# Queries, keys and values from three single-pass products of upper and lower parts instead of one full-precision product

## The reference

```
t = t + sliding_window_attention(_ln_t(t), Wq, Wk, Wv, Wo)   # 8 heads of 16, window 64
t = t + ternary_feed_forward(_ln_t(t), weight, bias)         # weight to its sign, output quantized
t = t + causal_attention(_ln_t(t), W_Q, W_K, W_V, W_O)       # 8 heads of 16
t = t + mixture_of_experts(_ln_t(t), ...)                    # 8 experts, 2 chosen for each token
```

## Time and profile before

| | |
|---|---|
| median of 3 runs | 248.85 us (248.84 to 248.93) |
| profiled execution | 249.03 us, of which the span is 247.2 us |
| TensorE busy (PE) | 230.5 us, 93% |
| VectorE busy (DVE) | 200.3 us, 81% |
| ScalarE busy (ACT) | 172.7 us, 70% |
| GpSimd busy (POOL) | 88.0 us, 36% |
| granted TensorE clock | full (2.4 GHz) throughout |

### The profile page before, as it was taken

One profiled execution on the slowest core, in us unless ns is written; L12 is line 12 of the kernel. 1 busy time (PEld: TensorE's weight loads), 2 busy tenths in 40 slices (PEclk: granted clock), 3 DMA queues, 4 the chain that ended last, 5 costly groups with the idle time before them and its releaser, 6 DMA issues.

```text
span 247.2 us, 4532 instructions
## 1 busy us (share of the span) xinstructions
PE 230.5 (93%) x1491; PEld 172.9 (70%) x1493; DVE 200.3 (81%) x524; ACT 172.7 (70%) x500; POOL 88.0 (36%) x155
## 2 busy tenths in 40 slices
PE   7999998899988989799897998999999999999993
PEld 2698666467765758466575666788888888888882
DVE  3677899966596897968799674889999996699885
ACT  2386455799698967998679976965855666666550
POOL 5200225988898556286288450002300000000000
PEclk9999999999999999999999999999999999999999
DMA  6910000004430300002000000510220002612001
GB/s 182 359 30 4 0 1 0 0 10 133 117 85 5 85 3 0 0 3 86 3 0 1 3 0 7 170 42 0 55 77 0 3 0 55 202 42 76 12 1 42
DMA packets 9318, 11.71 MB, mean 47 GB/s; under 512 B 704, under 2 KB 5952, under 8 KB 9168
## 3 DMA queue, kind: packets, MB, share of 16 engines
q1 hardware_dynamic: 8864, 11.09, 14.7%
q10 hardware_dynamic: 432, 0.33, 0.4%
HBM read 10.87 MB, written 0.56 MB: 46 GB/s over the span
## 4 chain that ended last, share of the span: by engine, by line
PE 62%; DVE 24%; ACT 8%; issue 2%; DMA 1%; POOL 1%; DVEq 0%; SPq 0%
PE bank L1006 6%; PE bank L1018 6%; PE bank L1007 6%; PE bank L1008 6%; PE bank L1019 6%; PE bank L1021 6%; DVE negmax L1146 5%; ACT early_prob L525 5%; PE bank L770 4%; PE bank L746 3%; PE bank L786 3%; DVE kM L1132 2%; DVE k_parts L1116 2%; DVE q_lo L1122 2%; PE bank L832 2%
## 5 line engine op out<-in xcount | busy, mean ns | idle before, releaser
L656 ACT ACTIVATE hb<-bank,pk 128x512 f32<-128x512 f32 x64 | 42.9, 706 | 20.6 <-PE bank L1008 20.6
L1401 DVE TENSOR_TENSOR hlo<-hb,hhi 128x512 fp32r<-128x512 f32 x64 | 43.1, 696 | 8.1 <-ACT hhi L659 7.0
L1146 DVE TENSOR_REDUCE negmax<-bank 128x2 f32<-128x384 f32 (+2 forms) x48 | 30.4, 641 | 13.0 <-PE bank L752 12.9
L525 ACT ACTIVATE prob<-bank,negmax 128x192 f32<-128x192 f32 (+1 forms) x64 | 28.2, 454 | 3.9 <-DVE negmax L1146 3.5
L486 ACT ACTIVATE probT<-bank 128x512 f32<-128x512 f32 x38 | 22.7, 610 | 4.3 <-PE bank L770 2.9
L1006 PE MATMUL bank<-xhi,w_hi 128*128 128x512 f32 x64 | 25.3, 396 | 0.0
L375 POOL TENSOR_TENSOR rstd<-ve,neghalf 128x2 f32<-128x2 f32 x16 | 11.4, 724 | 38.7 <-DVE ve L1103 38.7
L1018 PE MATMUL bank<-hhi,w_hi 128*128 128x512 f32 x64 | 25.1, 392 | 0.0
L1008 PE MATMUL bank<-xhi,w_lo 128*128 128x512 f32 x64 | 25.0, 390 | 0.0
L1007 PE MATMUL bank<-xlo,w_hi 128*128 128x512 f32 x64 | 25.0, 390 | 0.0
L1019 PE MATMUL bank<-hhi,w_lo 128*128 128x512 f32 x64 | 24.9, 389 | 0.0
(11 more groups left out here) (154 smaller groups left out, 516.8 us busy)
## 6 DMA issues: line engine op xcount, KB each, us to landing
w_raw<-w SPq DMA_DIRECT2D x16, 256.0 KB, 3.1
comb_b<-routes SPq DMA_DIRECT2D x16, 256.0 KB, 3.4
pk<-packed SPq DMA_DIRECT2D x1, 1280.0 KB, 8.4
pk<-packed SPq DMA_DIRECT2D x1, 560.0 KB, 5.7
xs<-x SPq DMA_DIRECT2D x3, 128.0 KB, 2.7
out<-acc SPq DMA_DIRECT2D x3, 128.0 KB, 1.7
xs<-x ACTq DMA_DIRECT2D x1, 128.0 KB, 2.9
out<-acc ACTq DMA_DIRECT2D x1, 128.0 KB, 1.8
```

The source lines that it names most:

```text
L525: last = nc.scalar.activation(prob_of(n, u)[:, of], lane[n][u % 2][:, of], ACT.Exp, bias=negmax[n][:, unit_query(u), h:h + 1], accum_out=s ...
L656: nc.scalar.activation(hb[blk % 2][:, j, :], h_bank[j][:, :], ACT.Relu, bias=bias).then_inc(h_ready, 1)
L1146: V.tensor_reduce(negmax[n][:, unit_query(u), heads[0]:heads[-1] + 1], lane[n][u % 2][:, :].rearrange("q (h k) -> q h k", h=len(heads))[:, ...
L1401: V.tensor_tensor(hlo[blk % 2][:, j, :], hb[blk % 2][:, j, :], hhi[blk % 2][:, j, :].bitcast(F32), ALU.subtract).then_inc(hlo_ready, 1)
```

## The change

1. The six projection weights leave `pk` and get a transfer of their own into a tile `projections` (128 x 2 x 640, 655 KB), on the SyncE queue behind the constants and ahead of the experts' weights.
2. GpSimd splits them into `p_hi` and `p_lo` in eight instructions of 128x320 between the group-norm powers of the first and of the second stage, waiting for the new transfer.
3. ScalarE's `turned` writes, for j = 0 and 2, the rounded tile `h_hi` in place of hT.
4. VectorE gets `lower_normed(a, n)`: bank minus h_hi, written to `h_lo`, 128x256, eight times. In phase 0 two stand around the copying of tokens 2 and 3, and two behind the first `largest` of both inputs (for inputs 2 and 3); in phases 2 and 3 two stand behind the last norm and ahead of `inverse_sums`.
5. TensorE's `project` does three F32R products for each full-precision one, 24 instead of 16 instructions for a pair, the third of each waiting for `h_lo`; the very first also waits for the split weights. `values` does three in place of one.
6. hT becomes two buffers instead of four; the first turn of probabilities in phase 0 waits for `h_low_ready` where it waited for `lnT_ready`.

```diff
@@ memory and loading
+        projections = sb("projections", [128, 2, QKV], scope=first_memory)
+        h_hi = each("h_hi", [128, T], F32R, n=2, scope=attention_memory)
+        h_lo = each("h_lo", [128, T], F32R, n=2, scope=attention_memory)
+        p_hi = each("p_hi", [128, QKV], F32R, n=2, scope=attention_memory)
+        p_lo = each("p_lo", [128, QKV], F32R, n=2, scope=attention_memory)
+            sp.dma_start(projections[:, :, :], packed[:, PACKED:].rearrange("p (a w) -> p a w", a=2)).then_inc(projections_in, 16)
@@ GpSimd
+            def split_projections(a):
+                for i in range(2):
+                    of = slice(i * QKV // 2, (i + 1) * QKV // 2)
+                    G.tensor_copy(p_hi[a][:, of], projections[:, a, of]).then_inc(p_upper, 1)
+                    pool.wait_ge(p_upper, 2 * a + i + 1)
+                    G.tensor_tensor(p_lo[a][:, of], projections[:, a, of], p_hi[a][:, of].bitcast(F32),
+                                    ALU.subtract).then_inc(p_ready, 1)
             for j in range(2):
+                if j == 1:
+                    pool.wait_ge(projections_in, 16)
+                    for a in range(2):
+                        split_projections(a)
                 for p, ns in enumerate(PAIRS):
@@ ScalarE, turned
-                copy(hT[n][:, :], norm_bank(j, n)[:, 0:T]).then_inc(lnT_ready, 1)
+                copy((h_hi[n % 2] if j in (0, 2) else hT[n % 2])[:, :], norm_bank(j, n)[:, 0:T]).then_inc(lnT_ready, 1)
@@ TensorE
             def project(a, n):
                 pe.wait_ge(lnT_ready, normed(2 * a, n))
-                for dst, w in ((lane[n][1], A_WK[a]), (lane[n][0], A_WQ[a])):
-                    for g in range(2):
-                        last = mm(dst[:, g * T:(g + 1) * T], w[:, g * 128:(g + 1) * 128], hT[n][:, :],
-                                  start=True, stop=True)
-                    last.then_inc(aqk_full, 1)
+                if a == 0 and n == 0:
+                    pe.wait_ge(p_ready, 4)
+                for bank_at, at in ((lane[n][1], WK_AT), (lane[n][0], WQ_AT)):
+                    projected(bank_at, a, n, at).then_inc(aqk_full, 1)
+            def projected(bank_at, a, n, at):
+                for g in range(2):
+                    upper, lower = parts_of(a, at + g * 128, at + (g + 1) * 128)
+                    sums = bank_at[:, g * T:(g + 1) * T]
+                    mm(sums, upper, h_hi[n % 2][:, :], start=True, stop=False)
+                    mm(sums, lower, h_hi[n % 2][:, :], start=False, stop=False)
+                    pe.wait_ge(h_low_ready[n], a + 1)
+                    last = mm(sums, upper, h_lo[n % 2][:, :], start=False, stop=True)
+                return last
             def values(a, n):
                 pe.wait_ge(k_parts_ready, a * B + n + 1)
+                upper, lower = parts_of(a, WV_AT, WV_AT + 128)
                 for i in range(TT):
-                    last = mm(lane[n][1][:, i * 128:(i + 1) * 128], hT[n][:, i * 128:(i + 1) * 128], A_WV[a],
-                              start=True, stop=True)
+                    of = slice(i * 128, (i + 1) * 128)
+                    mm(lane[n][1][:, of], h_hi[n % 2][:, of], upper, start=True, stop=False)
+                    mm(lane[n][1][:, of], h_hi[n % 2][:, of], lower, start=False, stop=False)
+                    last = mm(lane[n][1][:, of], h_lo[n % 2][:, of], upper, start=False, stop=True)
@@ turn_probs
-                    pe.wait_ge(lnT_ready, normed(0, other(n)))
+                    pe.wait_ge(h_low_ready[other(n)], 1)
@@ VectorE
+            def lower_normed(a, n):
+                dve.wait_ge(lnT_ready, normed(2 * a, n))
+                V.tensor_tensor(h_lo[n % 2][:, :], norm_bank(2 * a, n)[:, 0:T], h_hi[n % 2][:, :].bitcast(F32),
+                                ALU.subtract).then_inc(h_low_ready[n], 1)
             norm(0, 1)
+            lower_normed(0, 0)
             tokens(PAIRS[1])
+            lower_normed(0, 1)
             norm_variance(PAIRS[1])
             for p, (a, ns) in enumerate(PHASES):
                 if p >= 2:
                     norm(2, ns[1])
+                    for n in ns:
+                        lower_normed(1, n)
                 if p:
                     for n in ns:
                         inverse_sums(PHASES[p - 1][0], other(n))
...
                 for n in ns:
                     copy_values(a, n)
                     largest(a, n, 0)
+                if p == 0:
+                    for n in PAIRS[1]:
+                        lower_normed(0, n)
```

More of the change, by code:

```diff
@@ L29 @@
 BLOCKS = 2 * E
+QKV = 640
 RING = 4
@@ L37 @@
     group=128, vecs=8, wq=128, wk=128, wv=128, ident=128, wp=128, squeeze=96, conv=3 * 128,
-    aq=256, ak=256, av=128, ao=128, ident_bf=64, band0=64, band1=128, fw=128, fb=256, mean=128,
-    cq=256, ck=256, cv=128, co=128, causal0=64, causal1=128, headmask=8, router=8,
-    iota=8, b1=E * HC, b2=E,
+    ao=128, ident_bf=64, band0=64, band1=128, fw=128, fb=256, mean=128,
+    co=128, causal0=64, causal1=128, headmask=8, router=8,
+    iota=8, b1=E * HC, b2=E, aq=256, ak=256, av=128, cq=256, ck=256, cv=128,
 )
@@ L46 @@
     _at += _width
-PACKED = _at
+PACKED = AT["aq"]
 FIRST = AT["wq"]
-EARLY = AT["aq"]
+EARLY = AT["ao"]
 GAMMA, BETA, BQ, BK, BV, BP, BSQ, BCONV = range(8)
@@ L123, in build @@
         ht = each("ht", [128, TT, 128])
-        hT = each("hT", [128, T])
+        hT = each("hT", [128, T], n=2)
         fy = each("fy", [128, TT, 128], n=2)
@@ L216, in build @@
             sem(n) for n in ("av_full", "rb_ready", "rT_full", "rT_ready", "attn_ready", "wo_full", "t_ready"))
+        h_low_ready, p_upper, p_ready, projections_in = sems("h_low_ready"), sem("p_upper"), sem("p_ready"), sem("projections_in")
         unseen_zeroed = sems("unseen_zeroed")
@@ L235, in build, with parts_of @@
         y_full, yc_ready, acc_ready = sem("y_full"), sem("yc_ready"), sem("acc_ready")
-        A_WQ, A_WK, A_WV, A_WO = ([const(f"{layer}{n}") for layer in "ac"] for n in "qkvo")
+        A_WO = [const(f"{layer}o") for layer in "ac"]
+        def parts_of(a, lo, hi):
+            return p_hi[a][:, lo:hi], p_lo[a][:, lo:hi]
+        WQ_AT, WK_AT, WV_AT = 0, 256, 512
         A_MASK = [[const(f"{kind}{i}").bitcast(BF16) for i in range(TT)] for kind in ("band", "causal")]
@@ L390, in lower_tokens @@
                 pool.wait_ge(lnT_ready, normed(3, n))
-                G.tensor_tensor(xlo[:, cols], hT[n][:, :], xhi[:, cols].bitcast(F32), ALU.subtract
+                G.tensor_tensor(xlo[:, cols], hT[n % 2][:, :], xhi[:, cols].bitcast(F32), ALU.subtract
                                 ).then_inc(xlo_ready, 1)
@@ L702, in product @@
                     if j == 1:
-                        last = mm(lane[n][2][:, T + i * 128:T + (i + 1) * 128], hT[n][:, i * 128:(i + 1) * 128],
+                        last = mm(lane[n][2][:, T + i * 128:T + (i + 1) * 128], hT[n % 2][:, i * 128:(i + 1) * 128],
                                   w_eff[:, :], start=True, stop=True)
                     else:
-                        last = mm(logits_at(n)[:, i * E:(i + 1) * E], hT[n][:, i * 128:(i + 1) * 128],
+                        last = mm(logits_at(n)[:, i * E:(i + 1) * E], hT[n % 2][:, i * 128:(i + 1) * 128],
                                   const("router"), start=True, stop=True)
@@ L1506 @@
         mean=np.full((128, 128), 1.0 / C / C, f32),
-        cq=twice(a["L3_attn_W_Q"].reshape(128, 128).T), ck=twice(a["L3_attn_W_K"].reshape(128, 128).T),
-        cv=a["L3_attn_W_V"].reshape(128, 128).T, co=paired_rows(a["L3_attn_W_O"].T),
+        co=paired_rows(a["L3_attn_W_O"].T),
         causal0=mask(causal[0][:, 0:128]), causal1=mask(causal[1]),
@@ L1512 @@
         b1=a["L3_ffn_b1"].reshape(E * HC, 128).T, b2=a["L3_ffn_b2"].T,
+        aq=twice(a["L2_attn_Wq"].T), ak=twice(a["L2_attn_Wk"].T), av=a["L2_attn_Wv"].T,
+        cq=twice(a["L3_attn_W_Q"].reshape(128, 128).T), ck=twice(a["L3_attn_W_K"].reshape(128, 128).T),
+        cv=a["L3_attn_W_V"].reshape(128, 128).T,
     )
```

1 line of the change is left out of this document (removed).

## The result

The changed kernel takes 251.68 us (median of 4 runs, 251.60 to 251.72), the kernel before 248.84 (4 runs, 248.80 to 248.93): a ratio of 1.011 [1.0095, 1.0125], 2.84 us slower. The prediction was 251.1, range 249.2 to 253.8, slower with a chance of 0.80. The profiled execution took 251.68 us and has a span of 249.9 (247.2 before), so the two traces differ by 2.7.

What follows compares the result with a forecast made beforehand. VectorE's full stretches at attention phase boundaries were taken as the bound. Terms 0.4 + 0.85 + 0.6 + 0.6 - 0.2 gave +2.25 us, so 251.1 us was predicted, range 249.2 to 253.8.

Steps and rivals of the forecast that it cites:

- The bound: Attention phase boundaries: VectorE's full stretches set the end, so work put there counts and TensorE savings inside do not.
- The rival that TensorE bounds: Whole kernel: cheaper key and query products count and VectorE's work is hidden, -1.1, 247.8 us; chance 0.08.
- the rival of slack: VectorE's insertions: absorbed by later idle time, with phase 1's saving paying for the rest, 249.0 us; chance 0.12.
- The cost of a single-pass product: TensorE keys, queries and values: 0.11 us per instruction, so a key bank takes 0.18 less.
- The rival of values at four passes: TensorE values: six instructions of 0.22 us per input, +2.3 on top of the sum, 253.4 us; chance 0.20.
- Phase 0, start (+0.85): VectorE before phase 0's first lower_keys: two subtractions of 0.42 us for inputs 0 and 1 delay it by 0.85.
- Phase 0, after the first maximum (+0.6): VectorE between unit 0's and unit 1's maxima: two more subtractions, 0.84 less 0.24, delay it by 0.6 us.
- the same 0.24: Phase 0: gap between VectorE's maxima merge ending at 48.53 and ScalarE's unit-1 early_prob at 48.77, subtracted from 0.84.
- Phases 2 and 3 (+0.33, +0.3): VectorE before lower_keys: subtractions wait for ScalarE's copies with inverse_sums behind, +0.33 and +0.3, together +0.6 us.
- Phase 1 (-0.2): Phase 1 start, where VectorE idled for k_parts: the shorter first key bank counts in full, -0.2 us.
- The first part (+0.4): First 25 us: GpSimd's weight split meets VectorE's first_probs on SBUF, +0.4 us, bounds 0 and 1.2.

Runs made afterwards that it cites:

- no_lower_inputs: The changed kernel without VectorE's eight lower-part subtractions of the inputs and the product that reads them: 248.81 us, ratio 0.9985 to the kernel before.
- one_product: The changed kernel with all subtractions but only one of three products for keys and queries: 251.87 us, ratio 1.0124 to the kernel before.
- load_only: The kernel before with the six projection weights moved to a tile and transfer of their own, nothing split: 249.04 us, ratio 1.0004.
- split_only: The kernel before with the separate weight transfer and GpSimd's eight splitting instructions, whose results nothing reads: 249.12 us, ratio 1.0007.
- changed_again: The changed kernel run once more with no edit: 251.28 us, ratio 1.0095 to the kernel before.
- maxima_first: The changed kernel with phase 0's subtractions for inputs 2 and 3 each moved behind its lane's unit-1 maximum: 254.85 us, ratio 1.0227 to the kernel before.
- inverse_between: The changed kernel with the two inverse_sums of phases 2 and 3 put between the two subtractions: 250.87 us, ratio 1.0074 to the kernel before.
- clock_kept: The changed kernel with seven bf16 products of zeroes in TensorE's two gaps of phase 0: 251.73 us, ratio 1.0117 to the kernel before.
- between_kept: The changed kernel with seven zero products in phase 0's TensorE gaps and inverse_sums between the subtractions in phases 2 and 3: 250.68 us, ratio 1.0063.
- split_late: The changed kernel with GpSimd waiting for first_probs of inputs 0 and 1 before it splits the weights: 251.51 us, ratio 1.0095 to the kernel before.
- the second set: Four variants, the unedited changed kernel (251.28 us) among them, run on one chip with the kernel before at 248.97 us (11 runs).

## Why the prediction was right

**The bound.** Right. Taking VectorE's subtractions away, with the product that reads them, returned all of the loss (no_lower_inputs); taking away two of the three products for keys and queries and leaving the subtractions returned none (one_product), though there two falls of the clock hid 0.36 us of gain. The rival that TensorE bounds, 247.8 us, is dead by both, in spite of 93% busy. So is the rival of slack, 249.0: the subtractions stand on the chain.

**The cost of a single-pass product.** Right within a tenth: 0.12 us at 256 columns (0.11 taken, so a bank is 0.13 shorter by these distances and not 0.18) and 0.11 at 128. The rival of values at four passes, 253.4, falls by the three rows at 42.76 to 42.98. The loads last 0.19 and are 0.11 apart, so length was the wrong thing to price by and distance the right one, as the prediction read from the earlier trace rows. The rule of the Trainium skill that it weighed (TensorE: Matmul & The Clock Gate, section LDWEIGHTS: 107 ns for 128 columns) is the one that held as a pace: 0.11 and 0.12 us were measured.

**Phase 0, start (+0.85).** Measured +0.83, and 0.84 taken back by no_lower_inputs.

**Phase 0, after the first maximum (+0.6).** +0.46. Two subtractions in a row take 0.66 on the chain, not 0.84: the second starts 0.33 behind the first, before the first has ended by the profile. Less the same 0.24 that makes 0.42. The term was priced by the length of one operation (attnT, 416 ns), the mistake that the prediction avoided for weight loads; two attnT in a row took 0.75 us in the trace of before, not 0.83, and what follows them starts 0.66 behind the first.

**Phases 2 and 3 (+0.33, +0.3).** +0.36 and +0.31, and the experiment that puts the inverse_sums back into the wait gave 0.61 of it back. That the cost lay in the wait ahead of the inverse_sums and not in the subtraction itself is shown.

**Phase 1 (-0.2).** -0.25 up to K1 and then +0.25 up to E1, which the prediction didn't have. Of the -0.25, 0.16 is the shorter key bank; the other 0.09 stands ahead of the first key product of phase 1 (14.67 us behind E0 before, 14.58 after), so a little of phase 0's delay was caught up on the way. The +0.25 is a kM that started while GpSimd was splitting experts' weights. That the whole of it comes from there is read from rows of all twelve traces, though no kernel was run to move GpSimd alone. In phase 1:

| trace | what GpSimd's instruction still had to run when kM started | kM, in place of 0.69 | K1 to E1 |
|---|---|---|---|
| before, load_only, split_only, no_lower_inputs | at most 0.05 | 0.69 | 7.20 |
| one_product | 0.38 | 0.92 | 7.43 |
| the changed kernel | 0.38 | 0.93 | 7.45 |
| changed_again | 0.30 and 0.38 | 0.84 and 0.93 | 7.59 |
| maxima_first | 0.68 | 1.23 | 7.76 |

(inverse_between, clock_kept and between_kept are as the changed kernel, split_late has 7.49.) What kM lost is each time about 0.15 less than what GpSimd still had to run, and K1 to E1 is 7.20 plus what the kM lost, within 0.02. So the term depends on where GpSimd stands when VectorE arrives, and a change anywhere ahead of phase 1 can set it to nothing or double it. The Trainium skill (SBUF — State Buffer, section SBUF: two separate sides) says that a VectorE operation with two inputs in SBUF and a GpSimd one that reads SBUF exclude each other for the whole of an instruction, the one that starts first going first. The rows fit in kind: kM has both inputs in SBUF and was held up by what had started before it; the q_lo behind it, with one operand in a PSUM bank, took 0.69 beside GpSimd's next subtraction. In size the loss is the 0.15 smaller, and a kM that started 0.16 us into GpSimd's rstd (128x2, with 0.52 still to run, at 42.58 in the changed kernel) took its 0.69 as if alone.

**The first part (+0.4).** Over-sized as a price of the split, which costs 0.15 at the median (split_only). VectorE's four operations are stretched, but by 0.86 us in all in the first trace (0.34 to 1.44 in the others) and not by the 2.0 that the prediction worked out before it allowed for slack; GpSimd's rounding took 0.45 to 0.52 and its subtraction 0.86, where 0.52 and 0.93 were reckoned. N comes at 36.44 us (load_only) and 36.87 (before) without the split and at 36.69 to 37.82 in ten profiled executions with it (mean 37.2). So part of the +0.70 of the first trace is this spread.

**Where errors cancelled.** From N on the terms make +1.88 and the trace +1.97. That is closer than the terms are, and by luck: phase 0 was taken 0.14 too high behind the first maximum, and the 0.25 of phase 1 was not foreseen. The total of +2.25 stands 0.6 below the measured 2.84: about 0.3 lies in the first 37 us, 0.1 behind them, and 0.2 in the profiled execution of the kernel before, which was that much slower than its median.

**What the sum lacked** is the clock. The prediction took it as full throughout, from a page that showed it so, and in the profiled execution of the result it was. In other executions of the changed kernel it falls in phase 0: once for about 7 us, at a cost of 1.1 us (changed_again), once for half as long, at no cost (split_late). Before it fell, TensorE had waited 1.29 us between the values of inputs 0 and 1; in the kernel before that wait is 0.69. In no_lower_inputs it is 1.51 and the clock fell too, though k_parts comes no later there than before. So TensorE being done sooner with its banks is enough to lengthen the wait. Products that filled it kept the clock up in all six runs, which supports the wait as the cause. Why the clock stays up in one execution and falls in another behind the same wait is not shown.

**Open.** The runs of the result gave +2.84 and the second set +2.3, with the same kernel. The clock doesn't explain it: the four runs of the result lie within 0.12 us at clock shares from 0.990 to 0.999. The spread of the first part could, but only one execution of each kernel has a trace. Nor is it known why the time outside the span grows with the zero products.

## What to carry to other kernels

Price a new operation on the engine whose own queue fills the stretch where it is put, and not on the one whose products get cheaper: here taking out eight subtractions of 0.42 us and the product that reads them gave 2.5 to 2.9 us back, and taking out two products of three without them gave nothing. Take the price from distances between starts on every engine, VectorE too. Put work that waits for another engine first and let work that waits for nothing fill the wait behind it (0.61 us back), but look at who waits for the moved operation on an in-order engine before moving it (one such move cost 3.6 us). Where a change makes TensorE wait longer for others, look at its granted clock in several executions: one page at full speed doesn't show that it stays there.

## What the runs showed of the hardware

- The granted clock fell to 0.50 after TensorE had been idle for only 1.29 us, and stayed there for about 7 us in which TensorE was busy nearly all the time (changed_again). In the first trace of the same kernel, with the same wait of 1.29 us, it did not fall at all.
- Of VectorE and GpSimd the one that starts first is the one that keeps its time. A kM of 0.69 us that started while GpSimd's subtraction had 0.38 or 0.68 us to run took 0.93 or 1.23; where kM was first it took 0.69 and GpSimd's 0.73 became 1.16. A pair of prob operations, 0.62 us alone, took 0.77 to 1.57 beside GpSimd's split.
- Two VectorE subtractions of 128x256 with one operand in PSUM last 0.41 us each and start 0.33 apart.
- GpSimd rounds 128x320 in 0.45 us and subtracts 128x320 in 0.86.
